# Setup order of a recommender kernel: the rest of W1 behind the first X0 transposes, VectorE one pair tile ahead, and chunk 1's gathers spaced by landings

## The chip, the cores and the metric

The kernel runs on one core of a Trainium2 chip. Its time is device microseconds, taken without a profile; the version before has three such runs. A trace was taken of one further, profiled execution. Engines are named as the profile names them: PE (TensorE matrix products), PEld (its weight loads), DVE (VectorE), ACT (ScalarE), POOL (GpSimd) and SP (SyncE, which here only issues transfers). `ACTq` and `SPq` are instructions with which ACT and SP issue transfers.

## The reference

1024 samples have 39 ids each, and each id picks a row of 16 values from one of 39 tables. Two interaction layers follow, whose sums over the 16 dimensions go with a third through a small network:

```python
def _cin_layer(X0, Xi, W, b):
    Wr = W.reshape(H, F0_, Fi)
    return jnp.einsum('hjk,bjd,bkd->bhd', Wr, X0, Xi) + b[None, :, None]
X0 = embedded_features                     # (1024, 39, 16), gathered from the tables
Xi = X0
for W, b in [(W0, b0), (W1, b1), (W2, b2)]:
    Xi = _cin_layer(X0, Xi, W, b)          # 128 maps
    res.append(Xi.sum(axis=2))
z = jnp.concatenate(res, axis=1)
h = jnp.concatenate([z, dense_ctx], axis=1)
h = jnp.maximum(h @ W_top1 + b_top1, 0.0)
h = jnp.maximum(h @ W_top2 + b_top2, 0.0)
y = h @ W_top3
```

The third layer is needed only as its sum over the dimensions, and the kernel forms it without the full product.

## The kernel before

The samples come in 8 chunks of 128. Every matrix product runs as three with operands split into an upper and a lower part (`_hi`, `_lo`): ACT rounds a value to the upper part, and DVE or POOL subtracts that to get the lower one.

**Setup.** POOL gathers chunk 0: 39 indirect transfers (L458), one per field, into `e_in`; `gathered` counts 16 per landing. SP loads W0 and W1. PE transposes W1 in ten pieces of 512 columns (`w1_turned`, L945) through `ring`, four banks of PSUM; ACT takes each piece's upper part (`w1_upper`, L552) and DVE its lower part (`w1_lower`, L773). Seven tiles of W0 are treated the same way. The semaphores `setup_ps`, `setup_hi` and `setup_lo` count finished batches, 12 in all (`SETUP`): two of W0's tiles, ten of W1.

**Step -1** makes layer 0 of chunk 0's first half. ACT moves the gathered rows into `e_both` (L583, L584), which also frees `e_in` (`e_mid_ready`). PE transposes X0 in four parts (L1048); ACT evacuates each to `x0_t` (L622, `x_t` in the trace) and signals `x0t_ready`. Copies of `x0_t` are then laid out by transfers: three into `x0_rep` (issued by ACT, L669) and 20 for seven pair tiles (issued by SP, L355; four slots for these first tiles, later two). For each of the seven pair tiles, DVE multiplies (L831, `pair_made`), ACT takes the upper part (L603, `pair_hi`), DVE the lower (L836, `pair_lo`), and PE adds six products to `l0_ps` (L984 to L986). ACT's `x1_half` (L573) then writes `x1_hi` and raises `x1_hi_ready`; DVE adds `x1_lo` (L803). The loops over 16 dimensions d and 10 groups g only set the order: a step's work stands at its (d, g), as `MADE_MID` = 1 and `LO_MID` = 7 do for DVE's two operations and `HI_AT` = 7 for ACT's.

**Steps 0 to 7** run layer 1 for one chunk each: per dimension ten groups of three products (L1098 to L1100) into the four banks of `ring`, emptied in turn by ACT (L692) and DVE (L897). Beside that run the pair tiles still due, of which POOL makes tiles 7 and up: `multiply_pairs` (L489) and `lower_pairs` (L500). In step 0 DVE makes tile 7 of chunk 0, and POOL starts with tile 8. PE adds tile 8's products at group 3 and 5 of dimension 1.

**Gathers ahead.** POOL also gathers the following chunk. The table `GATHERS` spreads 39 gathers over the dimensions of a step. In step -1 no POOL product stands between them, so POOL issues 29 for chunk 1 back to back once `e_in` is free (`next_index`, L475); the ten left over come in step 0 as 3, 3, 2, 2.

Each engine runs its instructions in the order written; an instruction that waits holds back all behind it on its engine. Semaphores connect the engines.

Of the kernel before, what the change touches and what calls it, by code (L numbers as in the profile page):

```python
# [4 lines left out]
FIELDS, D, H = 39, 16, 128  # L5
# [4 lines left out]
def build_tower(nc, dense_ctx, ids, tables, W_top1, b_top1, W_top2, b_top2, W_top3, W0, b0, W1, b1, W2, b2, out):  # L10
    f32, f32r, i32 = mybir.dt.float32, mybir.dt.float32r, mybir.dt.int32
# [76 lines left out]
    FIRST_MADE = 7  # L88
# [34 lines left out]
    X2_WRITES = {13: 0, 2: 1, 6: 2}  # L123
    X2_LAST_AFTER, X0_AFTER = 9, 11
    X2_SLOTS = 8
    W1_PIECE, W1_FIRST = 2, 2
    W2_AT = ((10, 6), (11, 1), (11, 6), (12, 1), (12, 6), (13, 1), (13, 6), (14, 1), (14, 6), (15, 1))
    W2_OUT_AT = [(d, g + 3) for d, g in W2_AT]
    QUARTERS = 4
# [2 lines left out]
    with ctx:  # L132
# [323 lines left out]
        def _(pool):  # L456
# [15 lines left out]
            def step(c, odd, layer1, following, previous, mlp, gathers):  # L472
                def next_index():
                    pool.wait_ge(gathered, 16 * FIELDS * (c + 2))
                    nc.gpsimd.tensor_copy(idx[:, :], ids_sb[:, c + 2, :]).then_inc(idx_ready, 1)  # L475
                    pool.wait_ge(idx_ready, c + 3)
                    pool.wait_ge(e_mid_ready, c + 2)

                def multiply_pairs(chunk, i):

                    half, t = TILE[i]
                    n = TILES * chunk + i
                    rows = ROWS_OF[t]
                    products, loaded, count = pair_slot(chunk, i)
                    if isinstance(chunk, int) and chunk == 0 and i == PAIR_TILES + 1:
                        pool.wait_ge(pair_made, n)
                    after(pool, rep_in, 16 * PER_TILE * (2 * chunk + half + 1))
                    after(pool, loaded, count)
                    nc.gpsimd.tensor_tensor(products[0:rows, :], x0_rep[0:rows, :], products[0:rows, :],  # L489
                                            ALU.mult).then_inc(pair_made, 1)  # L490

                def lower_pairs(chunk, i):

                    n = TILES * chunk + i
                    rows = ROWS_OF[TILE[i][1]]
                    if isinstance(chunk, int) and chunk == 0 and i == PAIR_TILES + 1:
                        pool.wait_ge(pair_lo, n)
                    after(pool, pair_hi, n + 1)
                    after(pool, pair_used, n - 1)
                    nc.gpsimd.tensor_tensor(pairs_lo[0:rows, i % 2, :], pair_slot(chunk, i)[0][0:rows, :],  # L500
                                            pairs_hi[0:rows, i % 2, :].bitcast(f32),
                                            ALU.subtract).then_inc(pair_lo, 1)

                def make_block(g):
                    n = G_GROUPS * (c - 1) + g
                    if g == 0:
                        after(pool, xb_in, 16 * c)
                        pool.wait_ge(own_made, 3)
                    after(pool, g_ps, n - min(g, BLOCK_SLOTS - 1))
                    shape = [P, FIELDS, SAMPLES_PER_G]  # L510
                    nc.gpsimd.tensor_tensor(  # L511
                        blocks[:, g % BLOCK_SLOTS, 0:FIELDS, :],
                        xb[:, g, :].unsqueeze(2).to_broadcast(shape),
                        own[:, :].unsqueeze(1).to_broadcast(shape), ALU.mult).then_inc(block_made, 1)

                for d in range(D):
                    made = tile_made(c, d, layer1, following) if layer1 else None
                    if made:
                        multiply_pairs(*made)
                    if layer1 and following and d < INDEX_SLICE:  # L520
                        for f in range(FIELDS - LATE + sum(GATHERS[:d]), FIELDS - LATE + sum(GATHERS[:d + 1])):
                            gather(c + 1, f)
                    if gathers and d == INDEX_SLICE - 1:
                        next_index()
                    if gathers and d >= INDEX_SLICE:
                        for f in range(sum(GATHERS[INDEX_SLICE:d]), sum(GATHERS[INDEX_SLICE:d + 1])):
                            gather(c + 2, f)
                    if previous:
                        for r in range(G_GROUPS):
                            if G_AT[r][0] == d + 1:  # L530
                                make_block(r)
                    if layer1 and d == Z0_ADD_SLICE:
                        pool.wait_ge(z0_summed, 2 * (c + 1))
                        nc.gpsimd.tensor_tensor(z0[:, odd, :], z0_part[:, :], z0[:, odd, :],
                                                ALU.add).then_inc(z0_ready, 1)
                    if made:
                        lower_pairs(*made)
# [7 lines left out]
        def _(act):  # L545
# [11 lines left out]
            for q in range(SETUP_V):  # L557
# [4 lines left out]
                    last = nc.scalar.activation(v_hi[0:rows, t, :], ring[0:rows, batch % RING, i * H:(i + 1) * H],  # L562
                                                ACT.Copy)
                last.then_inc(setup_hi, 1)
            for q in range(W1_FIRST, GROUPS):
                w1_upper(q)

            def step(c, odd, layer1, following, previous, mlp, gathers):
# [55 lines left out]

                def side_work(d, g):

                    if following and layer1 and not previous and (d, g) in W2_OUT_AT:
                        q = W2_OUT_AT.index((d, g))
                        n = piece_width(q)
                        act.wait_ge(w2_ps, q + 1)  # L630
                        nc.scalar.activation(w2_t[:, BANK * q:BANK * q + n], side[:, q % 2, 0:n],
                                             ACT.Copy).then_inc(w2_ready, 1)
# [98 lines left out]
                act.wait_ge(y_ps, CHUNKS)  # L731
                nc.scalar.activation(y_row, side[0:1, 1, 0:P], ACT.Copy).then_inc(y_ready, 1)

            act.wait_ge(small_in, 48)
            act.wait_ge(bias_sums, 3)
            act.wait_ge(top_in, 96)
            steps(act, step, tail)

        @block.vector
        def _(dve):  # L740
# [38 lines left out]
            for t in range(PAIR_TILES):  # L779
# [6 lines left out]
                                               v_hi[0:rows, t, :].bitcast(f32), ALU.subtract)  # L786
                if t % 4 == 3 or t == PAIR_TILES - 1:
                    last.then_inc(setup_lo, 1)
            for q in range(W1_FIRST, GROUPS):
                w1_lower(q)  # L790
            dve.wait_ge(small_in, 48)
            nc.vector.tensor_scalar(b0_sum[:, :], b0_col[:, :], float(D), None, ALU.mult).then_inc(bias_sums, 1)
# [5 lines left out]
            def step(c, odd, layer1, following, previous, mlp, gathers):  # L798
# [8 lines left out]
                def z0_half(half):  # L807
# [3 lines left out]
                    else:  # L811
# [3 lines left out]
                        by_group(dst), l0_ps[:, :].rearrange("p (d b g) -> p b g d", b=SAMPLES_PER_G, g=G_GROUPS),  # L815
                        AX.X, ALU.add).then_inc(z0_summed, 1)

                def first_pairs(d, g):

                    made = tile_made(c, d, layer1, following)  # L820
                    made_at, lo_at = (8, 9) if d == D - 1 else (MADE_MID, LO_MID)
                    if made and g in (made_at, lo_at):
                        chunk, i = made
                        n = TILES * chunk + i
                        half, t = TILE[i]
                        rows = ROWS_OF[t]
                        products, loaded, count = pair_slot(chunk, i)
                        if g == made_at:
                            after(dve, rep_in, 16 * PER_TILE * (2 * chunk + half + 1))
                            after(dve, loaded, count)  # L830
                            nc.vector.tensor_tensor(products[0:rows, :], x0_rep[0:rows, :], products[0:rows, :],  # L831
                                                    ALU.mult).then_inc(pair_made, 1)
                        else:
                            after(dve, pair_hi, n + 1)
                            after(dve, pair_used, n - 1)
                            nc.vector.tensor_tensor(pairs_lo[0:rows, i % 2, :], products[0:rows, :],  # L836
                                                    pairs_hi[0:rows, i % 2, :].bitcast(f32),
                                                    ALU.subtract).then_inc(pair_lo, 1)

                def sum_terms(e, part):  # L840

# [16 lines left out]
                def side_work(d, g):  # L858
                    for half, chunk in halves(c, layer1, following):
                        if (d, g) == X1_LO_AT[half]:  # L860
                            x1_lower(chunk, half)
                    for half in range(2):
                        if layer1 and (d, g) == Z0_AT[half]:
                            z0_half(half)
                    if not layer1:
                        first_pairs(d, g)

                for d in range(D):
# [62 lines left out]
        def _(pe):  # L931
# [20 lines left out]
            for q in range(SETUP_V):  # L952
# [5 lines left out]
                    last = nc.tensor.transpose(ring[0:rows, batch % RING, i * H:(i + 1) * H], v_raw[:, x:x + rows],  # L958
                                               ident[:, :])
                last.then_inc(setup_ps, 1)  # L960
            for q in range(W1_FIRST, GROUPS):
                w1_turned(q)
            pe.wait_ge(top_in, 96)
            pe.wait_ge(bias_sums, 2)
# [5 lines left out]
            def step(c, odd, layer1, following, previous, mlp, gathers):  # L970
# [18 lines left out]

                def side_work(d, g):  # L990

                    for j in range(FIELDS):
                        if not previous or Z2_PLACES[j] != (d, g):
                            continue
# [84 lines left out]
                    if used and g in L0_AT[d]:  # L1079
                        layer0(*used, L0_AT[d].index(g) * BANK)  # L1080

                for d in range(D):
                    if layer1 and d % (D // 2) == 0:
                        k = 2 * c + d // (D // 2) + 1
# [18 lines left out]

            pe.wait_ge(bias_sums, 3)
            pe.wait_ge(e_cleared, 1)
            pe.wait_ge(setup_hi, SETUP)
            pe.wait_ge(setup_lo, SETUP)
            def tail():
                m = M1 // P - 1
                for k, z in enumerate((z0[:, CHUNKS % 2, :], g_t[:, FIELDS, :], z2_sb, dense_t[:, :])):  # L1110
# [91 lines left out]
```

## Time and profile before

| | us |
|---|---|
| three timed runs | 1361.97, 1360.40, 1358.06 |
| their median | 1360.4 |
| span of the profiled execution | 1393.5 |
| PE busy in that span | 1272.0 (91%) |
| DVE busy | 1087.9 (78%) |
| ACT busy | 1039.8 (75%) |
| POOL busy | 882.6 (63%) |

The profiled execution has no timed number of its own; its span, from the first to the last instruction, is 33.1 us above the median of the timed runs. In the page's strip of 40 slices the granted TensorE clock reads 7556 in the first four (tenths of full speed, a slice is 34.8 us) and 9 or more after; POOL's gathers fill its first three slices.

In the trace, `<-issue` behind an idle time means that nothing in the trace released the instruction, and `<-remote` that a semaphore did whose writer the trace does not name. A timeline row gives the start, the duration, the operation and, in brackets, the idle time before it on that engine and what ended it. PE durations overlap, so the pace of PE is read from the starts.

### The profile page before, as it was taken

The page shows a single profiled execution, that of the slowest core. Times are in us where ns is not written, and L with a number is a line of the kernel's source. Part 1 is how long each engine was busy: PE and PEld are TensorE (multiplying, and loading weights), DVE is VectorE, ACT ScalarE, POOL GpSimd, SP SyncE. Part 2 cuts the span into 40 slices and gives each one's busy share as a digit, 9 for nine tenths or more (in the row PEclk, how much of TensorE's full clock was granted, in tenths as well). Part 3 has the DMA queues.
Part 4 walks back from the last instruction along what each step waited for, and adds up shares of the span by engine and source line. Part 5 has one row for each costly group of instructions (what it writes and reads, how often), then busy time and mean ns, then how long its engine had stood idle before and what let it go on. Part 6 is the DMA issues. An engine that isn't in the chain of part 4 may idle for free.

```text
span 1393.5 us, 23236 instructions
## 1 busy us (share of the span) xinstructions
PE 1272.0 (91%) x6037; PEld 1041.9 (75%) x6037; DVE 1087.9 (78%) x2694; ACT 1039.8 (75%) x3353; POOL 882.6 (63%) x654
## 2 busy tenths in 40 slices
PE   2127999999999999999999999999999999999997
PEld 2115778777888878787887878787888888887876
DVE  3125898988888788888888888888888888988992
ACT  1114888888788887788777877888778887788772
POOL 6572777786776867686776877686776745363000
PEclk7556999999999999999999999999999999999999
DMA  4042522242233221242223221242232221240000
GB/s 147 10 107 56 139 63 62 75 99 52 62 75 89 57 58 48 68 100 52 65 72 82 57 67 48 68 96 56 56 81 78 58 64 46 65 98 25 16 16 16
DMA packets 71598, 92.39 MB, mean 66 GB/s; under 512 B 31745, under 2 KB 53762, under 8 KB 70306
## 3 DMA queue, kind: packets, MB, share of 16 engines
q1 hardware_dynamic: 61318, 87.75, 24.5%
q0 software_dynamic: 9984, 2.58, 2.0%
q8 instruction: 53, 0.87, 0.3%
q14 instruction: 87, 0.71, 0.2%
q10 hardware_dynamic: 156, 0.48, 0.1%
HBM read 21.03 MB, written 10.95 MB: 23 GB/s over the span
## 4 chain that ended last, share of the span: by engine, by line
PE 81%; DVE 5%; ACT 4%; another core or an unknown queue 4%; issue 4%; DMA 1%; ACTq 0%; POOL 0%; DVEq 0%; SPq 0%; POOLq 0%
PE ring L1098 19%; PE ring L1100 19%; PE ring L1099 18%; PE side L998 4%; PE side L1065 4%; PE l_ps L984 4%; PE l_ps L986 3%; PE l_ps L985 3%; ACT terms L692 2%; DVE x_s L852 2%; DVE terms L897 2%; PE side L1017 1%; PE side L1048 1%; PE side L1026 1%
## 5 line engine op out<-in xcount | busy, mean ns | idle before, releaser
L692 ACT ACTIVATE terms<-ring,e_both 128x128 f32<-128x128 f32 x2944 | 839.2, 403 | 214.4 <-PE ring L1100 180.2
L1098 PE MATMUL ring<-w_hi,x_hi 128*128 128x512 f32 (+1 forms) x1280 | 556.5, 435 | 15.8 <-ACT terms L692 8.7
L897 DVE SCALAR_TENSOR_TENSOR terms<-ring,e_both,terms 128x128 f32<-128x128 f32 x1792 | 507.9, 344 | 65.2 <-PE ring L1100 57.3
L1100 PE MATMUL ring<-w_hi,x_lo 128*128 128x512 f32 (+1 forms) x1280 | 499.1, 390 | 0.0
L1099 PE MATMUL ring<-w_lo,x_hi 128*128 128x512 f32 (+1 forms) x1280 | 497.2, 388 | 0.0
L852 DVE TENSOR_REDUCE x_s<-terms 128x32 f32<-128x800 f32 x512 | 489.1, 976 | 0.7 <-ACT terms L692 0.7
L500 POOL TENSOR_TENSOR pairs_lo<-pairs,pairs_hi 117x1024 fp32r<-117x1024 f32 (+1 forms) x104 | 250.1, 2404 | 231.7 <-ACT pairs_hi L603 226.7
L458 POOL DMA_INDIRECT e_in<-in_tbl,idx x312 | 302.1, 968 | 93.8 <-issue 70.6
L1098 PEld LDWEIGHTS ring<-w_hi,x_hi 128*128 128x128 f32 x1280 | 242.9, 190 | 74.4 <-ACT terms L692 17.7
L1100 PEld LDWEIGHTS ring<-w_hi,x_lo 128*128 128x128 f32 x1280 | 241.1, 188 | 50.5
L489 POOL TENSOR_TENSOR pairs<-x_rep,pairs 117x1024 f32<-117x1024 f32 (+1 forms) x104 | 250.3, 2406 | 36.4 <-DMA pairs<-x_t 35.4
L1099 PEld LDWEIGHTS ring<-w_lo,x_hi 128*128 128x128 f32 x1280 | 243.6, 190 | 39.3
L603 ACT ACTIVATE pairs_hi<-pairs 117x1024 fp32r<-117x1024 f32 (+1 forms) x109 | 119.9, 1100 | 23.8 <-issue 14.8
L889 DVE SCALAR_TENSOR_TENSOR terms<-ring,e_both,b_rows 128x128 f32<-128x128 f32 x128 | 44.9, 350 | 117.4 <-PE ring L1100 116.9
L984 PE MATMUL l_ps<-pairs_hi,v_hi 117*128 117x512 f32 (+1 forms) x224 | 95.2, 425 | 43.9 <-DVE pairs_lo L836 20.9
L998 PEld LDWEIGHTS side<-g_t,w_t 128*128 128x128 f32 x546 | 100.3, 188 | 22.3
L998 PE MATMUL side<-g_t,w_t 128*128 128x128 f32 x546 | 102.2, 273 | 0.0
L511 POOL TENSOR_TENSOR blocks<-xb,own 128x312 f32<-128x312 f32 x112 | 79.6, 731 | 26.3 <-PE side L1065 23.4
L986 PE MATMUL l_ps<-pairs_lo,v_hi 117*128 117x512 f32 (+1 forms) x224 | 90.9, 406 | 0.0
L985 PE MATMUL l_ps<-pairs_hi,v_lo 117*128 117x512 f32 (+1 forms) x224 | 90.8, 405 | 0.0
L984 PEld LDWEIGHTS l_ps<-pairs_hi,v_hi 117*128 117x128 f32 (+1 forms) x224 | 43.5, 194 | 59.3 <-issue 26.6
L1065 PE MATMUL side<-blocks,x_r 128*128 128x320 f32 x224 | 79.0, 434 | 0.1
(113 smaller groups left out, 655.8 us busy)
## 6 DMA issues: line engine op xcount, KB each, us to landing
pairs<-x_t SPq DMA_DIRECT2D x312, 156.0 KB
x_scratch<-x_s SPq DMA_DIRECT2D x32, 256.0 KB, 2.2
x_r<-x_scratch SPq DMA_DIRECT2D x7, 1024.0 KB
x_rep<-x_t SPq DMA_DIRECT2D x45, 156.0 KB
e_in<-in_tbl,idx POOLq DMA_INDIRECT x312
x_scratch<-e_both SPq DMA_DIRECT2D x8, 312.0 KB, 7.6
g_t<-in_L_rec_W SPq DMA_DIRECT2D x1, 2496.0 KB, 15.9
xb<-x_scratch SPq DMA_DIRECT2D x8, 312.0 KB
```

What stands on the lines that cost most here:

```text
L458: nc.gpsimd.indirect_dma_start(e_in[:, f, :], None, tables[f], bass.IndirectOffsetOnAxis(ap=idx[:, f:f + 1], axis=0)).then_inc(gathered, 16)
L489: nc.gpsimd.tensor_tensor(products[0:rows, :], x0_rep[0:rows, :], products[0:rows, :], ALU.mult).then_inc(pair_made, 1)
L500: nc.gpsimd.tensor_tensor(pairs_lo[0:rows, i % 2, :], pair_slot(chunk, i)[0][0:rows, :], pairs_hi[0:rows, i % 2, :].bitcast(f32), ALU.subt ...
L692: last = nc.scalar.activation(term(d, ACT_BEFORE[d][g] + i), twos(ring[:, (GROUPS * d + g) % RING, i * H:(i + 1) * H]), ACT.Copy, scale=sc ...
L852: last = nc.vector.tensor_reduce(twos(x2_s[:, d % X2_SLOTS, h]), terms[:, d % 2, a, 0:TERMS[d], :].rearrange("p a t b -> p a b t"), AX.X, ...
L897: nc.vector.scalar_tensor_tensor(out=acc, in0=y, scalar=scale_of(j, d), in1=acc, op0=ALU.mult, op1=ALU.add).then_inc(dve_unit, 1)
L984: nc.tensor.matmul(acc, v_hi[0:rows, t, :], p_hi, start=(t == 0), stop=False)
L998: last = nc.tensor.matmul(side[:, 0, 0:P], w2_t[:, j * H:(j + 1) * H], g_t[:, j, :], start=(j == 0), stop=(j == FIELDS - 1))
L1065: nc.tensor.matmul(side[:, r % 2, 0:SAMPLES_PER_G * GCOLS], x2_r[:, r, :], blocks[:, r % BLOCK_SLOTS, :, :].rearrange("p b j -> p (b j)"), ...
L1098: nc.tensor.matmul(acc, x1_hi[:, x], w1_hi[:, w], start=True, stop=False)
L1099: nc.tensor.matmul(acc, x1_hi[:, x], w1_lo[:, w], start=False, stop=False)
L1100: nc.tensor.matmul(acc, x1_lo[:, x], w1_hi[:, w], start=False, stop=True).then_inc(y_group, 1)
```

## The change

It edits the order of the setup in four places; the work itself stays, and no transfer or operation is added or removed.

W1's pieces 5 to 9 (transposes, uppers, lowers) move from the setup into step -1, to (6, 0): behind the first two X0 transposes and the layout transfers, ahead of the first pair tile. ACT's waits for the small inputs move there and to the start of step 0. PE's wait for all twelve setup batches moves to the start of step 0; ahead of step -1 it waits for seven.

DVE's order in step -1 becomes one tile ahead: product d, then the lower part of d - 1. POOL's 29 gathers in step -1 get waits: the first for `x0t_ready` (two parts evacuated), each of the first twelve for the landing of the one before, the thirteenth for `x1_hi_ready`.

```diff
@@ constants
-    W1_PIECE, W1_FIRST = 2, 2
+    W1_PIECE, W1_FIRST, W1_EARLY = 2, 2, 5
+    W1_REST_AT = (6, 0)
+    GATHERS_EARLY = 12
@@ POOL, step
                         for f in range(sum(GATHERS[INDEX_SLICE:d]), sum(GATHERS[INDEX_SLICE:d + 1])):
+                            if not layer1 and f == 0:
+                                pool.wait_ge(x0t_ready, 2)
+                            if not layer1 and f == GATHERS_EARLY:
+                                pool.wait_ge(x1_hi_ready, 1)
+                            if not layer1 and f < GATHERS_EARLY:
+                                pool.wait_ge(gathered, 16 * (FIELDS + f))
                             gather(c + 2, f)
@@ ACT (DVE with w1_lower and PE with w1_turned alike)
-            for q in range(W1_FIRST, GROUPS):
+            for q in range(W1_FIRST, W1_EARLY):
                 w1_upper(q)
...
+                    if not layer1 and (d, g) == W1_REST_AT:
+                        for q in range(W1_EARLY, GROUPS):
+                            w1_upper(q)
+                        act.wait_ge(small_in, 48)
+                    if layer1 and not previous and (d, g) == (0, 0):
+                        act.wait_ge(top_in, 96)
+                        act.wait_ge(bias_sums, 3)
...
-            act.wait_ge(small_in, 48)
-            act.wait_ge(bias_sums, 3)
-            act.wait_ge(top_in, 96)
             steps(act, step, tail)
@@ DVE, first_pairs
+                    if (d, g) == W1_REST_AT:
+                        for q in range(W1_EARLY, GROUPS):
+                            w1_lower(q)
+                    if g == MADE_MID and tile_made(c, d, layer1, following) and d < D - 1:
+                        first_product(d)
+                        if d > FIRST_MADE:
+                            first_lower(d - 1)
+                    if (d, g) == (FIRST_MADE + PAIR_TILES, 0):
+                        first_lower(d - 1)
+                    if (d, g) == (D - 1, 8):
+                        first_product(d)
+                    if (d, g) == (D - 1, 9):
+                        first_lower(d)
@@ PE
+                if layer1 and not previous:
+                    pe.wait_ge(setup_hi, SETUP)
+                    pe.wait_ge(setup_lo, SETUP)
...
-            pe.wait_ge(setup_hi, SETUP)
-            pe.wait_ge(setup_lo, SETUP)
+            pe.wait_ge(setup_hi, SETUP - GROUPS + W1_EARLY)
+            pe.wait_ge(setup_lo, SETUP - GROUPS + W1_EARLY)
```

`first_product` and `first_lower` hold the same two operations with the same waits that `first_pairs` had (L831, L836).

POOL, from its first index copy to tile 8's lower part, before. `e_in<-in_tbl,idx` is a gather; a number behind x counts equal instructions in a row.

```order
L467 COPY idx<-ids_sb 128x39 [waits ids_in]
L458 DMA e_in<-in_tbl,idx 128x16 [waits idx_ready]
L458 DMA e_in<-in_tbl,idx 128x16 x38
L475 COPY idx<-ids_sb 128x39 [waits gathered]
L458 DMA e_in<-in_tbl,idx 128x16 [waits e_mid_ready,idx_ready]
L458 DMA e_in<-in_tbl,idx 128x16 x28
L489 TENSOR_TENSOR pairs<-x_rep,pairs 117x1024 [waits pair_in0,rep_in,pair_made]
L458 DMA e_in<-in_tbl,idx 128x16 x3
L500 TENSOR_TENSOR pairs_lo<-pairs,pairs_hi 117x1024 [waits pair_used,pair_hi,pair_lo]
```

And now:

```order
L469 COPY idx<-ids_sb 128x39 [waits ids_in]
L460 DMA e_in<-in_tbl,idx 128x16 [waits idx_ready]
L460 DMA e_in<-in_tbl,idx 128x16 x38
L477 COPY idx<-ids_sb 128x39 [waits gathered]
L460 DMA e_in<-in_tbl,idx 128x16 [waits x0t_ready,gathered,e_mid_ready,idx_ready]
L460 DMA e_in<-in_tbl,idx 128x16 [waits gathered] x11
L460 DMA e_in<-in_tbl,idx 128x16 [waits x1_hi_ready]
L460 DMA e_in<-in_tbl,idx 128x16 x16
L491 TENSOR_TENSOR pairs<-x_rep,pairs 117x1024 [waits pair_in0,rep_in,pair_made]
L460 DMA e_in<-in_tbl,idx 128x16 x3
L502 TENSOR_TENSOR pairs_lo<-pairs,pairs_hi 117x1024 [waits pair_used,pair_hi,pair_lo]
```

The run of 29 gathers is split into 12 that wait for landings and 17 that stand between `x1_hi_ready` and tile 8's product (L489 before, L491 now). The three gathers between that product and its lower part stay.

ACT, from W1's later uppers to the first pair tiles, before:

```order
L552 ACTIVATE w_hi<-ring 128x512 [waits setup_ps] x7
L552 ACTIVATE w_hi<-ring 128x384 [waits setup_ps]
L583 ACTIVATE e_both<-e_in 128x624 [waits top_in,gathered,bias_sums,small_in]
L584 ACTIVATE e_both<-e_in 128x304
L622 ACTIVATE x_t<-side 58x512 [waits x0t_ps] x2
L669 DMA x_rep<-x_t 39x1024 [waits x0t_ready]
L669 DMA x_rep<-x_t 39x1024 x2
L603 ACTIVATE pairs_hi<-pairs 117x1024 [waits pair_made] x2
```

And now:

```order
L560 ACTIVATE w_hi<-ring 128x512 [waits setup_ps] x3
L591 ACTIVATE e_both<-e_in 128x624 [waits gathered]
L592 ACTIVATE e_both<-e_in 128x304
L630 ACTIVATE x_t<-side 58x512 [waits x0t_ps] x2
L684 DMA x_rep<-x_t 39x1024 [waits x0t_ready]
L684 DMA x_rep<-x_t 39x1024 x2
L560 ACTIVATE w_hi<-ring 128x512 [waits setup_ps] x4
L560 ACTIVATE w_hi<-ring 128x384 [waits setup_ps]
L611 ACTIVATE pairs_hi<-pairs 117x1024 [waits pair_made,small_in]
L611 ACTIVATE pairs_hi<-pairs 117x1024 [waits pair_made]
```

X0's move and its first two evacuations (L583, L622; now L591, L630) and the three layout transfers pass the last five uppers of W1.

DVE at the first pair tiles, before:

```order
L831 TENSOR_TENSOR pairs<-x_rep,pairs 117x1024 [waits pair_in0,rep_in]
L836 TENSOR_TENSOR pairs_lo<-pairs,pairs_hi 117x1024 [waits pair_hi]
L831 TENSOR_TENSOR pairs<-x_rep,pairs 117x1024 [waits pair_in1,rep_in]
L836 TENSOR_TENSOR pairs_lo<-pairs,pairs_hi 117x1024 [waits pair_hi]
L831 TENSOR_TENSOR x_r<-x_rep,x_r 117x1024 [waits pair_in2,rep_in]
L836 TENSOR_TENSOR pairs_lo<-x_r,pairs_hi 117x1024 [waits pair_used,pair_hi]
```

And now, with W1's last lowers ahead of them:

```order
L785 TENSOR_TENSOR w_lo<-ring,w_hi 128x512 [waits setup_hi] x4
L785 TENSOR_TENSOR w_lo<-ring,w_hi 128x384 [waits setup_hi]
L837 TENSOR_TENSOR pairs<-x_rep,pairs 117x1024 [waits pair_in0,rep_in]
L837 TENSOR_TENSOR pairs<-x_rep,pairs 117x1024 [waits pair_in1,rep_in]
L847 TENSOR_TENSOR pairs_lo<-pairs,pairs_hi 117x1024 [waits pair_hi]
L837 TENSOR_TENSOR x_r<-x_rep,x_r 117x1024 [waits pair_in2,rep_in]
L847 TENSOR_TENSOR pairs_lo<-pairs,pairs_hi 117x1024 [waits pair_hi]
L837 TENSOR_TENSOR x_r<-x_rep,x_r 117x1024 [waits pair_in3,rep_in]
```

Each product (L837) now stands ahead of the lower part (L847) of the tile before it.

## Rows read from the trace of the kernel before

**Rows 1.** The windows view: busy time of each engine by stretch of the span, in us.
```profile
core 0: us, PE busy (x) PEld busy (x) DVE busy (x) ACT busy (x) POOL busy (x), PEclk, DMA share, GB/s
67.10:126.00 58.90, 19.89 (x51) 13.43 (x51) 18.12 (x15) 9.59 (x11) 28.18 (x28) 0.56 0.35 83
126.00:142.00 16.00, 16.00 (x59) 12.86 (x60) 11.32 (x29) 11.19 (x37) 10.32 (x7) 0.82 0.31 79
142.00:1354.00 1212.00, 1191.78 (x5677) 978.95 (x5675) 1031.50 (x2559) 996.53 (x3254) 804.20 (x572) 1.00 0.27 66
```

**Rows 2.** Waits of PE, 142 to 1354 us: total us, times, longest.
```profile
PE ring L1098 <- ACT terms L692: 8.7, 15, 1.4
```

**Rows 3.** Waits of all engines, 0 to 130 us.
```profile
ACT w_hi L552 <- remote: 40.0, 6, 10.6
...
ACT x_t L622 <- remote: 19.4, 1, 19.4
```

**Rows 4.** Timeline, chunk 0's last gather to X0's move: start us, us, operation, [idle before].
```profile
51.96 0.95 POOL L458 DMA_INDIRECT e_in<-in_tbl,idx  x1 [0.30 <-issue]
54.31 0.22 POOL L475 COPY idx<-ids_sb 128x39 int32<-128x39 int32 x1 [1.40 <-DMA e_in<-in_tbl,idx]
...
63.33 0.72 ACT L583 ACTIVATE e_both<-e_in 128x624 f32<-128x624 f32 x1 [3.27 <-issue]
...
65.17 0.97 POOL L458 DMA_INDIRECT e_in<-in_tbl,idx  x1 [10.65 <-ACT e_both L584]
...
66.52 0.59 ACT L622 ACTIVATE x_t<-side 58x512 f32<-58x512 f32 x1 [0.26 <-PE side L1048]
```

**Rows 5.** Timeline of step -1: first tiles, SP's loads, second half of X0.
```profile
67.14 4.02 ACTq L669 DMA_DIRECT2D x_rep<-x_t  x3
...
78.18 1.23 DVE L831 TENSOR_TENSOR pairs<-x_rep,pairs 117x1024 f32<-117x1024 f32 x1 [14.94 <-issue]
79.44 1.06 ACT L603 ACTIVATE pairs_hi<-pairs 117x1024 fp32r<-117x1024 f32 x1 [12.33 <-issue]
80.53 1.26 DVE L836 TENSOR_TENSOR pairs_lo<-pairs,pairs_hi 117x1024 fp32r<-117x1024 f32 x1 [1.12 <-issue]
81.71 1.21 DVE L831 TENSOR_TENSOR pairs<-x_rep,pairs 117x1024 f32<-117x1024 f32 x1
...
87.74 0.61 PE L1048 MATMUL side<-ident,e_both 128*65 128x128 f32 x4
...
94.44 2.13 SPq L355 DMA_DIRECT2D x_r<-x_t  x2
...
107.15 0.59 ACT L622 ACTIVATE x_t<-side 58x512 f32<-58x512 f32 x1 [19.42 <-remote]
```

**Rows 6.** Timeline of POOL in step -1: a gather beside VectorE, and the last.
```profile
81.78 1.96 POOL L458 DMA_INDIRECT e_in<-in_tbl,idx  x1 [0.30 <-issue]
...
102.58 0.94 POOL L458 DMA_INDIRECT e_in<-in_tbl,idx  x1 [0.30 <-issue]
```

**Rows 7.** Timeline, the end of step -1 and the first groups of step 0.
```profile
123.40 1.11 ACT L573 ACTIVATE x_hi<-l_ps,b_col 128x1024 fp32r<-128x1024 f32 x1 [4.27 <-PE l_ps L986]
...
125.98 0.76 PE L1098 MATMUL ring<-w_hi,x_hi 128*128 128x512 f32 x1 [2.62 <-DVE x_lo L803]
...
130.76 2.46 POOL L489 TENSOR_TENSOR pairs<-x_rep,pairs 117x1024 f32<-117x1024 f32 x1 [27.24 <-DMA pairs<-x_t]
134.36 1.11 ACT L603 ACTIVATE pairs_hi<-pairs 117x1024 fp32r<-117x1024 f32 x1
...
135.31 1.98 ACT L692 ACTIVATE terms<-ring,e_both 128x128 f32<-128x128 f32 x7
...
137.54 0.39 PE L1098 MATMUL ring<-w_hi,x_hi 128*128 128x512 f32 x1
```

**Rows 8.** Timeline of step 0: the last late gather and what waits for it.
```profile
159.87 0.95 POOL L458 DMA_INDIRECT e_in<-in_tbl,idx  x1 [0.30 <-issue]
...
167.63 0.72 ACT L583 ACTIVATE e_both<-e_in 128x624 f32<-128x624 f32 x1 [2.90 <-DMA e_in<-in_tbl,idx]
```

More of the change, by code:

```diff
@@ L788, in _ @@
                     last.then_inc(setup_lo, 1)
-            for q in range(W1_FIRST, GROUPS):
+            for q in range(W1_FIRST, W1_EARLY):
                 w1_lower(q)
@@ L816, in z0_half @@
                         AX.X, ALU.add).then_inc(z0_summed, 1)
-                def first_pairs(d, g):
[L820 to L838, printed above, removed]
@@ new lines, in first_product @@
+                def first_product(d):
+                    chunk, i = tile_made(c, d, layer1, following)
+                    rows = ROWS_OF[TILE[i][1]]
+                    products, loaded, count = pair_slot(chunk, i)
+                    after(dve, rep_in, 16 * PER_TILE * (2 * chunk + TILE[i][0] + 1))
+                    after(dve, loaded, count)
+                    nc.vector.tensor_tensor(products[0:rows, :], x0_rep[0:rows, :], products[0:rows, :],
+                                            ALU.mult).then_inc(pair_made, 1)
@@ new lines, in first_lower @@
+                def first_lower(d):
+                    chunk, i = tile_made(c, d, layer1, following)
+                    n = TILES * chunk + i
+                    rows = ROWS_OF[TILE[i][1]]
+                    after(dve, pair_hi, n + 1)
+                    after(dve, pair_used, n - 1)
+                    nc.vector.tensor_tensor(pairs_lo[0:rows, i % 2, :], pair_slot(chunk, i)[0][0:rows, :],
+                                            pairs_hi[0:rows, i % 2, :].bitcast(f32),
+                                            ALU.subtract).then_inc(pair_lo, 1)
@@ L864, in side_work @@
                             z0_half(half)
-                    if not layer1:
+                    if not layer1 and following:
                         first_pairs(d, g)
@@ L960, in _ @@
                 last.then_inc(setup_ps, 1)
-            for q in range(W1_FIRST, GROUPS):
+            for q in range(W1_FIRST, W1_EARLY):
                 w1_turned(q)
@@ L990, in side_work @@
                 def side_work(d, g):
+                    if not layer1 and (d, g) == W1_REST_AT:
+                        for q in range(W1_EARLY, GROUPS):
+                            w1_turned(q)
                     for j in range(FIELDS):
```

## The prediction

> **What bounds the kernel now.** I read the windows by stage first. From 142 to 1354 us PE is busy 1191.78 of 1212.00 us at a granted clock of 1.00 [rows 1]; the largest wait of PE in it is 8.7 us in 15 pieces, for ACT's terms [rows 2]. The change touches nothing there, so those 1212 us stay. What it can move lies before 142 us: the stretch 67.1 to 126 us, where PE is busy 19.89 of 58.90 us, and the first 16 us of step 0, where PE has no idle time but a mean clock of 0.82.
>
> The table of waits names two long ones in the setup, both of ACT and both with a releaser that the trace does not name: 40.0 us before W1's uppers in six pieces, and 19.4 us before one evacuation of X0 [rows 3]. The timeline places them. Chunk 0's last gather lands by 54.31 us, and X0's move, which could have begun then, begins at 63.33 us because ACT still works off W1's uppers [rows 4]: 9.0 us. Later PE turns X0's third part at 87.74 to 88.35 us, and ACT takes it at 107.15 us [rows 5], 3.6 us after the last of 29 gathers was issued (102.58 + 0.94) [rows 6]. With only two gathers issued, the second evacuation came 0.26 us after it was free to, released by PE [rows 4]. In this trace, then, signals from PE to ACT come late while POOL issues many gathers in a row.
>
> The central question is whether the timed runs hold these waits. The profiled span is 33.1 us above the median. The two waits cost the span 9.0 and about 17.3 us (19.4 less the roughly 2 us that DVE's chain would have needed anyway), 26.3 in all. Nothing else before 142 us is as large, and a stretch with PE 98% busy leaves little room to be shorter unprofiled. I take it that most of the 33.1 us is these two waits, and that they belong to the profiled execution.
>
> Two sentences of the Trainium skill stand beside this, and the sum does without them. "Runtime: NRT & Kernel Launch", section "The ~15µs preamble/postamble breakdown", gives a profile total about 6.2 us more than the reported time, whatever the kernel; by it some 27 of the 33.1 us are left, close to my 26.3, though no row here shows that part. "NOTIFIC — the notification-queue block", section "7.1 Overflow: three behaviours, one of which stalls the engine", says that the unit which writes the records holds back its producers rather than lose one; by it a late signal could be the recording's own, which the trace agrees with as far as the late ones fall beside many gathers, and does not prove.
>
> **The change part by part**, as the timed runs would have it. S is the start of layer 1, 125.98 us in this trace [rows 7].
>
> *W1's last five pieces.* Moved behind the layout transfers, they need five uppers of 0.60 us, as many lowers and 19 transposes. ACT and DVE stand idle 12.3 and 14.9 us ahead of the first pair tile [rows 5], while the transfers land, so I cost the work at 0. If the cover were gone, five uppers would cost 3.0 us. What the move gains is the 9.0 us, and only where ACT really waits; without late signals ACT would have been done with W1 before the gathers landed. Taken 0, bounds 0 and -9.0.
>
> *One tile ahead.* Before, product to product takes 3.53 us (78.18 to 81.71): product 1.23, upper 1.06, lower 1.26. DVE alone needs 1.23 + 1.26 = 2.49, so six steps save at most 6 x 1.04 = 6.2 us. Against that, SP's last tile loads are issued at 94.44 to 96.57 us [rows 5]; from the first product on, the old chain without the long wait reaches the last product at 78.18 + 6 x 3.53 = 99.4 us, only 2.8 us later. What is late next is SP's loads. Bounds 0 and -6.2; I take -2.5, near the loads, since spaced gathers may let them go a little sooner.
>
> *The gathers' waits.* The first twelve now cost a landing each. A quiet one took 54.31 - 51.96 = 2.35 us [rows 4]; one in step 0 took 167.63 - 159.87 = 7.76 us [rows 8]. From the first one's release at 67.14 us to `x1_hi_ready` (124.51 in this trace [rows 7], less 17.3 and 2.5) are 37.6 us, or 3.1 us for each of twelve. Up to 3.1 us they hide entirely. I take that, being nearer to the quiet row; each us above it would move the rest back by 12 us. As lower bound stands 0, as upper bound 12 x 4.7 = 56 us, which I hold unlikely since in step 0 the landing shared the queues with more.
>
> Behind the thirteenth gather's wait for `x1_hi_ready` are sixteen more, then tile 8's product. `x1_hi_ready` comes at S - 1.47 (123.40 + 1.11). A gather takes 0.95 + 0.30 = 1.25 us of POOL [rows 4], so seventeen end at S - 1.47 + 21.25 = S + 19.8. The product needs 2.46 us: S + 22.2; before, it ended at S + 7.2 [rows 7]. ACT's upper of tile 8 waits for it, with the terms of dimension 0's group 7 behind it in ACT's order: 1.11 for the upper and 4/7 of 1.98, or 1.13, for the terms, so that bank is free at S + 24.6, hand-overs of 0.1 us among them. PE wants it for dimension 1's second group, which began at S + 11.56 (137.54) [rows 7]. PE stalls 13.0 us there, and all the terms, PE's main work and every later step with it. Nothing takes this back, since PE has no slack later [rows 1]. Were gathers cheaper unprofiled, by their 0.30 us of issue, seventeen would save 5.1 us: bounds 8 and 13.
>
> *The clock.* Where PE stood idle two thirds of the time, the granted clock was 0.56; in the 16 us that follow, 0.82 with PE busy throughout [rows 1], which costs 16 x 0.18 = 2.9 us. A stall of 13 us puts PE back into such a state: once more 2.9 us. Bounds 0 and 2.9; I take 2.9.
>
> *Waits put off* (`top_in`, `bias_sums`, the last setup batches) end long before step 0; 0.
>
> The trap that the Trainium skill names in "SBUF — State Buffer", section "SBUF: two separate sides", bears on the paced gathers: GpSimd cannot write a gather's descriptors while VectorE runs a two-port operation. The trace has a row for it, 1.96 instead of 0.95 us beside a VectorE product at 81.71 [rows 5, 6]; twelve such would lengthen the early part by 12 us, which the upper bound above contains.
>
> Sum: -2.5 + 13.0 + 2.9 = +13.4 us, against the median since no removed wait of the profile is in it: 1360.4 + 13.4 = 1373.8, or 1374 us. With its bounds (-6.2 + 8 + 0 up to 0 + 13 + 2.9, and half of twelve gathers 1 us late each) its own range is 1363 to 1384.
>
> **The rivals.**
>
> *The waits are in the timed runs too* (faster). Then -9.0 - 17.3 - 2.5 + 13.0 + 2.9, and since seventeen gathers still run in a row beside PE's first groups, ACT's terms come late by some 4 us more: -8.9 us, 1351 us, with 1346 to 1356 around it. For it: the trace shows them plainly, and a semaphore that is late holds ACT for real in that execution. Against it: 33.1 us would have no other home.
>
> *They cancel.* Half the waits, or gathers that cost POOL less and a one-ahead order worth its full 6.2 us, against the same stall: within 4 us of 1360. The two bounds nearest to zero, -6.2 and +8, leave +2.
>
> *The stall doesn't come.* If PE's group 1 of dimension 1 did not stand behind tile 8's upper, 26 to 29 us would be free with the waits real: 1333 us. The order of ACT speaks against it: the upper stands ahead of group 7's terms [rows 7].
>
> *The early gathers are slow* (slower still): at 4.1 us a landing the burst starts 12 us later and PE's stall grows to 25: 1386 us. It decides from 3.1 us a landing on. I hold it within the forecast's upper end.
>
> **How the numbers follow.** Forecast, with its slow tail, 0.56; the waits are real 0.26; they cancel 0.14; no stall 0.04. Of this kernel 0.3% (4.1 us) can be told from no change. Faster takes the second and the fourth, 0.30; within 0.3% the third, 0.14; slower the first, 0.56. The time is 1374; the range reaches down to the heart of the faster case, 1348, and up to the forecast's own end, 1384.
>
> **What the profile after would show.** X0's move soon after the landing at about 54 us, and no 19 us before the third evacuation, by either case; so its span may be shorter than 1393.5 us by 26.3 + 2.5 - 15.9 = 13 us even where the time is longer. That would be the plainest sign that the profile held waits that the timed runs do not. POOL: twelve gathers some 3 us apart, seventeen at 1.25 us from `x1_hi_ready`, then tile 8's product some 20 us behind layer 1's start. PE: one idle piece of about 13 us before dimension 1's group 1, ended by ACT's terms, and the clock low behind it. The forecast is wrong if that piece is under 5 us, or if the time falls by more than 4 us with it in place; then the unnamed waits are real.

## The result, and the profile after

The changed kernel takes 1382.0 us (median of four runs, 1380.52 to 1384.96), the kernel before 1359.2 us beside it: a ratio of 1.0173, with a 95% interval of 1.0150 to 1.0196. It is 22.8 us slower. The profiled execution ran 1380.52 us with a span of 1378.7 us, so its trace shows a normal run. The profiled span fell from 1393.5 us while the time rose, as the prediction said it might.

First the windows of the changed kernel, cut at 97.0 (just behind layer 1's first product on PE, which starts at 95.78), at the start and end of PE's idle piece (107.7, 131.8), and where the clock is back (140.0); columns as in [rows 1].

```profile
core 0: us, PE busy (x) PEld busy (x) DVE busy (x) ACT busy (x) POOL busy (x), PEclk, DMA share, GB/s
0.00:54.00 54.00, 8.21 (x35) 7.32 (x35) 10.92 (x62) 5.53 (x14) 37.94 (x46) 0.68 0.34 97
54.00:97.00 43.00, 22.63 (x80) 17.16 (x81) 20.84 (x20) 14.17 (x19) 9.80 (x10) 0.70 0.45 113
97.00:107.70 10.70, 10.66 (x37) 7.86 (x36) 7.76 (x19) 5.32 (x17) 4.64 (x5) 0.80 0.33 82
107.70:131.80 24.10, 0.05 (x1) 0.00 (x0) 0.00 (x0) 2.14 (x6) 19.05 (x19) 0.58 0.07 6
131.80:140.00 8.20, 8.19 (x27) 6.31 (x28) 5.39 (x13) 5.46 (x18) 7.42 (x6) 0.78 0.25 57
140.00:1378.70 1238.70, 1218.12 (x5860) 1004.89 (x5858) 1040.44 (x2581) 1005.12 (x3283) 801.77 (x571) 1.00 0.27 65
```

The fourth stretch is the loss: 24.1 us in which PE and DVE do nothing, ACT has 2.1 us of work, the transfer engines are busy 7%, and only POOL works, 19 us of it.

The waits of the changed kernel from 0 to 180 us name the chain backwards (total, times, longest):

```profile
POOL e_in L460 <- DMA e_in<-in_tbl,idx: 34.2, 11, 5.0
...
PE ring L1131 <- ACT terms L707: 26.9, 3, 24.1
ACT pairs_hi L611 <- POOL pairs L491: 25.4, 1, 25.4
```

PE waits for ACT's terms, ACT for POOL's product of tile 8, and POOL had waited for eleven landings (the thirteenth gather waits for `x1_hi_ready` alone, so the twelfth landing holds nothing). POOL's timeline of the changed kernel shows the last steps:

```profile
58.63 0.97 POOL L460 DMA_INDIRECT e_in<-in_tbl,idx  x1 [4.40 <-ACT x_t L630]
64.58 0.94 POOL L460 DMA_INDIRECT e_in<-in_tbl,idx  x1 [4.97 <-DMA e_in<-in_tbl,idx]
...
101.22 0.94 POOL L460 DMA_INDIRECT e_in<-in_tbl,idx  x1 [1.75 <-DMA e_in<-in_tbl,idx]
105.09 0.94 POOL L460 DMA_INDIRECT e_in<-in_tbl,idx  x1 [2.93 <-DMA e_in<-in_tbl,idx]
106.34 0.95 POOL L460 DMA_INDIRECT e_in<-in_tbl,idx  x1 [0.30 <-issue]
...
126.31 0.94 POOL L460 DMA_INDIRECT e_in<-in_tbl,idx  x1 [0.30 <-issue]
127.28 2.35 POOL L491 TENSOR_TENSOR pairs<-x_rep,pairs 117x1024 f32<-117x1024 f32 x1
```

Twelve gathers stand from 58.63 to 105.09 us, (105.09 - 58.63) / 11 = 4.2 us apart. Seventeen follow at 1.25 us, and tile 8's product comes behind them. ACT and PE answer at the other end, the changed kernel's rows for [rows 7]:

```profile
93.20 1.11 ACT L581 ACTIVATE x_hi<-l_ps,b_col 128x1024 fp32r<-128x1024 f32 x1 [3.00 <-PE l_ps L1013]
...
129.66 1.06 ACT L611 ACTIVATE pairs_hi<-pairs 117x1024 fp32r<-117x1024 f32 x1 [25.38 <-POOL pairs L491]
130.62 2.94 ACT L707 ACTIVATE terms<-ring,e_both 128x128 f32<-128x128 f32 x11
```

```profile
95.78 0.76 PE L1131 MATMUL ring<-w_hi,x_hi 128*128 128x512 f32 x1 [2.62 <-DVE x_lo L815]
...
131.81 0.80 PE L1131 MATMUL ring<-w_hi,x_hi 128*128 128x512 f32 x1 [24.05 <-ACT terms L707]
```

`x1_hi` was ready at 94.31 us, but the seventeen gathers began at 106.34 us: 12 us of the stall come from the landings, 12 from the burst behind them; the experiments below take the two apart.

### The profile page after: what moved, and what is told of

The parts are those of the page before. It is cut to its first block, busy times and chain, and to the rows that moved or that the text cites. A ratio compares the mean times of both kernels' runs of the same rounds, so it can differ in the third digit from the quotient of the medians.

```text
span 1378.7 us, 23238 instructions
## 1 busy us (share of the span) xinstructions
PE 1267.9 (92%) x6037; PEld 1043.5 (76%) x6037; DVE 1085.3 (79%) x2694; ACT 1037.7 (75%) x3353; POOL 880.6 (64%) x654
## 4 chain that ended last, share of the span: by engine, by line
PE 81%; DVE 5%; issue 2%; POOL 2%; DMA 1%; ACT 1%; SPq 0%; DVEq 0%; POOLq 0%
PE ring L1131 19%; PE ring L1133 19%; PE ring L1132 19%; PE side L1095 4%; PE side L1028 4%; PE l_ps L1011 4%; PE l_ps L1013 3%; PE l_ps L1012 3%; DVE x_s L879 2%; DVE terms L924 2%; PE side L1047 2%; PE side L1078 1%; POOL e_in L460 1%; PE side L1056 1%; PE side L1183 1%
## 5 line engine op out<-in xcount | busy, mean ns | idle before, releaser
L491 POOL TENSOR_TENSOR pairs<-x_rep,pairs 117x1024 f32<-117x1024 f32 (+1 forms) x104 | 249.9, 2403 | 10.9 <-DMA pairs<-x_t 10.0
L513 POOL TENSOR_TENSOR blocks<-xb,own 128x312 f32<-128x312 f32 x112 | 79.3, 729 | 25.5 <-PE side L1095 24.1
```

## The experiments

Eleven runs put three questions: whether the timed runs ever held the unnamed waits of [rows 3], which edit costs the time, and what is left to gain. The kernel before ran beside each: its median was 1361.1 us for the first four, 1359.2 us for the next four and 1358.4 us for the last three.

**Without the gathers of step -1.** The kernel before, without 28 of its gathers; the counts that wait for landings are lowered by 28 x 16 = 448 to match, so this kernel computes chunk 1 from what lies in the buffer.

```diff
-                            gather(c + 2, f)
+                            if layer1 or f == 0:
+                                gather(c + 2, f)
```

> The kernel before, without 28 of the 29 gathers of chunk 1 in step -1 (only the first stays; chunk 1 then uses what lies in the buffer, and the counts of landings are lowered to match). Theory 1, the unnamed waits of ScalarE belong to the profiled execution of before and the timed runs don't hold them: the time stays at 1356 to 1361 us. Rival, the timed runs hold the 19.4 us wait behind the gathers: it goes with them, and the time falls by 13 to 19 us, to 1340 to 1346 us. By both, the third evacuation of X0 comes without a long wait in this profile.

Measured: 1362.7 us, ratio 1.0009 (0.9990 to 1.0027). That is 1.7 us above the expected range, and 1.6 us above the kernel before beside it. No 19 us are there to go. Theory 1 holds.

**W1's move alone.** All edits on W1 and the waits put off, without those on DVE's order and on the gathers.

> The kernel before, with W1's last five pieces behind the first X0 transposes and the waits put off; VectorE's order and the gathers as before. Theory 1: ScalarE is done with W1 before the gathers land, so the time stays within 3 us of before, 1356 to 1362 us. Rival, the waits are in the timed runs: 9 us less, 1350 us.

Measured: 1359.5 us, ratio 0.9993 (0.9983 to 1.0004). Its profile has 29 gathers in a row, and still PE releases the third evacuation after 1.64 us and the fourth after 0.34 us. The wait of 19.42 us in [rows 5] stood before the fourth; the prediction and the expectations call it the third. The third of that first trace was this one:

```profile
85.66 0.59 ACT L622 ACTIVATE x_t<-side 58x512 f32<-58x512 f32 x1 [1.65 <-issue]
```

**The gathers' waits alone.** The hunk on POOL of the change, nothing else.

> The kernel before, with the gathers' waits alone (first for two evacuations, twelve for a landing each, the thirteenth for x1_hi). The stall of the changed kernel (24.05 us before dimension 1's second group, ended by ScalarE's terms) comes from these waits: it must be here too, 18 to 26 us long, less by what layer 1 starts later; time 1378 to 1386 us. Rival, part of the loss comes from W1's move or VectorE's order: the time is under 1373 us.

Measured: 1381.8 us, ratio 1.0162 (1.0136 to 1.0187), with a stall of 20.14 us at the same place. The waits carry the whole loss. `x1_hi` came 2.4 us later than in the changed kernel (95.57 against 93.20), and layer 1 with it, so less of the gathers' lateness showed as a stall, and the time is the same.

**W1's move and one tile ahead, no gathers' waits.**

> The changed kernel without the gathers' waits: W1's move and VectorE one tile ahead. From the changed kernel's time less its stall and clock, 1382.0 - 24.1 - 1.8 = 1356.1: 1353 to 1359 us, no stall before dimension 1's second group. Rival, without spaced gathers the late signals come back in timed runs: 1365 us or more. Rival, the waits of before were real and go here in part: 1345 us or less.

Measured: 1358.1 us, ratio 0.9977 (0.9962 to 0.9993); PE has no stall before dimension 1's second group. Its longest wait for ACT's terms between 85 and 175 us is 2.2 us, at 141.59 us; the kernel before has one of 2.7 us at 144.19 us in its second profile.

**The kernel before, profiled again.**

> The kernel before, unchanged, profiled once more. Theory 1a, the unnamed waits of ScalarE belong to that one profiled execution: this one is without them, its span is 1356 to 1360 us, X0's move begins at about 54 us and the third evacuation at about 76 us, as in the run with W1's move alone. Theory 1b, every profiled execution of this order of work holds them: a span of 1390 us or more beside a time of 1360 us.

Measured: a span of 1360.4 us, 0.4 us beyond the expected range, at a time of 1363.3 us. The timeline of ACT in this second profile, to be held against 63.33 and 107.15 us in [rows 4, 5]:

```profile
54.10 0.72 ACT L583 ACTIVATE e_both<-e_in 128x624 f32<-128x624 f32 x1 [34.67 <-DMA e_in<-in_tbl,idx]
...
75.95 0.59 ACT L622 ACTIVATE x_t<-side 58x512 f32<-58x512 f32 x1 [1.39 <-PE side L1048]
...
78.05 0.59 ACT L622 ACTIVATE x_t<-side 58x512 f32<-58x512 f32 x1
...
96.44 1.11 ACT L573 ACTIVATE x_hi<-l_ps,b_col 128x1024 fp32r<-128x1024 f32 x1 [4.31 <-PE l_ps L986]
```

X0's move starts with the landing. The third evacuation is released by PE, and the fourth, at 78.05 us, follows without idle time; it is the one to hold against 107.15 us. No wait `<-remote` is left in this trace. POOL's rows of the same profile show that the gathers were as dense as ever, and where tile 8's product stood:

```profile
71.08 0.95 POOL L458 DMA_INDIRECT e_in<-in_tbl,idx  x1 [0.30 <-issue]
72.33 1.96 POOL L458 DMA_INDIRECT e_in<-in_tbl,idx  x1 [0.30 <-issue]
...
97.15 0.95 POOL L458 DMA_INDIRECT e_in<-in_tbl,idx  x1 [0.30 <-issue]
103.90 2.47 POOL L489 TENSOR_TENSOR pairs<-x_rep,pairs 117x1024 f32<-117x1024 f32 x1 [5.80 <-DMA pairs<-x_t]
```

The last early gather ends at 98.10 us; the product waits for a transfer, not for gathers.

**Nine gathers that wait instead of twelve.**

```diff
-    GATHERS_EARLY = 12
+    GATHERS_EARLY = 9
```

> The changed kernel with 9 in place of 12 gathers that wait for a landing each, so 20 behind x1_hi. Theory: twelve landings of 3.9 us (58.63 to 105.09 us in the changed kernel's trace) end 11 us after x1_hi is there (94.31), and hold the rest of the gathers and tile 8's product back. Nine end before it; the rest runs from 94.3 us on, 20 x 1.25 = 25.0, so the product starts at 119.3 instead of 127.28 us: PE's stall 24.05 - 8.0 = 16 us, time 1374 us (1371 to 1377). Rival, the number of gathers behind x1_hi alone sets the stall: three more gathers, 3.8 us more, 1386 us.

Measured: 1377.4 us (1371.33 to 1380.36), ratio 1.0118 (1.0081 to 1.0155). Three more gathers stood behind `x1_hi`, and the time fell; the rival would have it rise. POOL and PE of this kernel:

```profile
93.00 0.94 POOL L460 DMA_INDIRECT e_in<-in_tbl,idx  x1 [3.14 <-DMA e_in<-in_tbl,idx]
94.95 0.94 POOL L460 DMA_INDIRECT e_in<-in_tbl,idx  x1 [1.01 <-ACT x_hi L581]
...
120.33 2.35 POOL L491 TENSOR_TENSOR pairs<-x_rep,pairs 117x1024 f32<-117x1024 f32 x1
```

```profile
124.86 0.80 PE L1131 MATMUL ring<-w_hi,x_hi 128*128 128x512 f32 x1 [17.45 <-ACT terms L707]
```

The tenth gather waits for `x1_hi`, not for a landing. The product comes 7.0 us earlier than in the changed kernel and the stall is 6.6 us shorter. The time is at the upper end of what was expected, 0.4 us beyond it.

**Every second gather waits, two in flight.**

```diff
-                            if not layer1 and f < GATHERS_EARLY:
+                            if not layer1 and f < GATHERS_EARLY and f % 2 == 0:
```

> The changed kernel with only every second of the twelve early gathers waiting for the landings before it, two in flight. The early part is over before x1_hi; seventeen gathers from 94.3 us on end at 115.6 us, so the product starts 11.7 us earlier than in the changed kernel and PE's stall is 12.3 us, near the 13.0 of the prediction's sum; time 1370 us (1367 to 1373). Rival, two in flight land twice as late each: no change, 1382 us.

Measured: 1371.7 us (1369.57 to 1379.44), ratio 1.0103 (1.0058 to 1.0149). The thirteenth gather starts when `x1_hi` is there, and PE's stall is close to the 13.0 us of the prediction's sum:

```profile
96.06 0.94 POOL L460 DMA_INDIRECT e_in<-in_tbl,idx  x1 [0.36 <-ACT x_hi L581]
...
117.00 2.35 POOL L491 TENSOR_TENSOR pairs<-x_rep,pairs 117x1024 f32<-117x1024 f32 x1
```

```profile
121.53 0.80 PE L1131 MATMUL ring<-w_hi,x_hi 128*128 128x512 f32 x1 [13.10 <-ACT terms L707]
```

**Without the wait for `x1_hi`.**

> The changed kernel without the thirteenth gather's wait for x1_hi. Theory: that wait is long met when the twelfth has been issued (x1_hi at 94.31, the twelfth gather at 105.09 us), so nothing changes: a stall of 24 us, time 1382 us (1379 to 1385). Rival, the wait for x1_hi is what holds the gathers: 10 us less or more, 1372 us or below.

Measured: 1383.7 us, ratio 1.0190 (1.0157 to 1.0223), stall 24.0 us: no change, since the landings end later anyway.

Six kernels in one table, with PE's stall before dimension 1's second group in the profiled execution: without its stall, each time is within 2.5 us of 1359.2 us, the median of the kernel before beside the change.

| kernel | PE's stall, us | time, us | difference |
|---|---|---|---|
| no gathers' waits | 0 | 1358.1 | 1358.1 |
| every second of twelve | 13.1 | 1371.7 | 1358.6 |
| nine | 17.45 | 1377.4 | 1359.9 |
| twelve, without the other edits | 20.1 | 1381.8 | 1361.7 |
| twelve, no wait for `x1_hi` | 24.0 | 1383.7 | 1359.7 |
| the change | 24.05 | 1382.0 | 1358.0 |

**What is left to gain.** Three kernels without the landings' waits ran side by side.

> W1's move and VectorE one tile ahead, of the gathers' waits only the first (for two evacuations), 29 gathers back to back behind it. They start 2.7 us later than without it (58.6 instead of 55.9 us) and end at about 101 us; tile 8's product waited for its transfer until 103.9 us in the clean profile of before, so nothing is held back. Theory: as with no wait at all, 1355 to 1360 us, no stall. Rival, every wait on these gathers costs what it delays: 2.7 us more than without.

> The kernel before with VectorE one tile ahead alone. Theory: of the two edits that are left without the gathers' waits, this one carries all the gain, 1.4 us at x1_hi (95.01 against 96.44 us): 1356 to 1360 us, the same as with W1's move within 2 us. Rival, W1's move carries it: no gain here, 1360 us or more, 2 us above the run with both.

> W1's move and VectorE one tile ahead, the gathers as before, once more with five rounds: the candidate for a version that beats both. Theory: 1 to 4 us less than before, 1355 to 1359 us, interval of the ratio below 1. Rival, the first result was chance: ratio 1.000 with 1 inside the interval.

Measured: with the first wait kept 1357.5 us, ratio 0.9996 (0.9983 to 1.0010); one tile ahead alone 1357.3 us, 0.9991 (0.9980 to 1.0003); both edits without waits 1355.8 us, 0.9982 (0.9970 to 0.9994). The last is the version that beats both kernels, by 0.2%, and did so twice. Whether W1's move adds to it can't be told: alone neither edit differs from before, and the three intervals overlap. For the same reason the theory that one tile ahead carries all the gain is not shown, nor is a cost of the first wait ruled out: its kernel's median lies 1.6 us above the one without waits, between the theory's 0 and the rival's 2.7.

## Why the prediction was right, point by point

The direction was right, and so was the chain by which the time is lost: gathers in front of tile 8's product, ACT's terms behind it, PE's stall. The size was not: +13.4 us was forecast, +22.8 us measured. That 1382.0 us still lies in the range is partly luck. By the range's own terms its ends are 1360.4 - 6.2 + 8 = 1362.2 and 1360.4 + 15.9 + 6 = 1382.3 us, not 1363 and 1384, and the rival "the early gathers are slow", which is what took place, was priced at 1386 us, beyond the end that was said to hold it.

**The central question** came out as taken: the timed runs don't hold the unnamed waits. The runs without gathers (1362.7 us) and with W1 moved (1359.5 us) show it in the time, the second profile of before in the trace. The rival by which they were real (1351 us) is ruled out, and with it the late evacuation's 17.3 us and X0's 9.0 us as gains.

What the prediction said of their nature does not hold. It saw them where POOL issues many gathers in a row. Six more profiles (before again, W1 alone, one tile ahead alone, and the three with both edits and no waits for landings) have 29 gathers in a row and no late signal, and none of the twelve profiles taken after the first has a wait `<-remote`. They belonged to one execution. The sentence of the Trainium skill in "NOTIFIC — the notification-queue block", section "7.1 Overflow: three behaviours, one of which stalls the engine", remains a possible cause that no run here shows; recording alone does not bring the waits, since the second profile was recorded too. Their cause stays open.

The 6.2 us of the Trainium skill's "Runtime: NRT & Kernel Launch", section "The ~15µs preamble/postamble breakdown", are said of a profile's total, and no run here shows that quantity. The prediction set them against a span from the first to the last instruction, and there they did not serve: the time is longer than the span, by 1.8 us in the changed kernel's profiled run (1380.52 against 1378.7).

**W1's pieces at 0**: confirmed, ratio 0.9993. In the changed kernel they ran at 61.4 to 65 us, while the layout transfers landed.

**One tile ahead at -2.5**, with SP's loads late next: the last product moved from 89.83 us in the second profile of before to 87.40 us with both edits and no waits, and the start of `x1_hi` from 96.44 to 95.01 us, 1.4 us. The same kernel profiled again had it at 93.69 us, 2.8 us sooner; the 2.5 taken lies between. DVE's order in the first of these two profiles shows who is late now:

```profile
75.02 1.23 DVE L830 TENSOR_TENSOR x_r<-x_rep,x_r 117x1024 f32<-117x1024 f32 x1 [1.45 <-DMA x_r<-x_t]
...
81.36 1.23 DVE L830 TENSOR_TENSOR pairs<-x_rep,pairs 117x1024 f32<-117x1024 f32 x1 [1.40 <-DMA pairs<-x_t]
...
85.12 1.23 DVE L830 TENSOR_TENSOR pairs<-x_rep,pairs 117x1024 f32<-117x1024 f32 x1 [1.40 <-DMA pairs<-x_t]
```

The products wait for tile loads. Whether spaced gathers let these go sooner is not shown: with them `x1_hi` began at 93.20 us (the change), 93.57 us (nine) and 94.29 us (no wait for `x1_hi`), without them at 93.69 to 95.01 us in four profiles with one tile ahead.

**The burst of seventeen gathers at 13.0 us** was right in place and size: 13.1 us where the early part was over in time, each gather 1.25 us. Nothing was taken back later that the table above could show.

**The landings are the term that was mis-sized.** Taken was 3.1 us each, near the quiet row of [rows 4], which hid all twelve. Measured are 4.2 us from one gather to the next, between that and the 7.76 us of [rows 8]. From the first gather's release to `x1_hi` were 35.7 us (58.63 to 94.31), which eleven landings of 3.1 us and one gather fill; the early part ended 12 us later. The text had the price nearly right, 12 us for each us above 3.1 (eleven landings make it 11), and this case as its slow end ("at 4.1 us a landing ... PE's stall grows to 25").

The nearest row was the wrong choice. In the quiet row's window the transfer engines were busy 8%; the early gathers run beside 20 tile loads, with the engines busy 49% from the first to the twelfth. The changed kernel's windows, cut from one gather to the next, show that the landing goes with this load:

```profile
58.63:64.58 5.95, 2.47 (x13) 1.84 (x11) 2.51 (x5) 2.45 (x5) 0.97 (x2) 0.79 0.65 159
...
85.49:88.17 2.68, 1.33 (x5) 1.11 (x6) 2.68 (x4) 1.06 (x1) 0.97 (x1) 0.91 0.03 3
```

With the engines busy 65% the next gather came after 5.95 us, with 3%, in a gap of SP's loads, after 2.68 us. The nine between took 3.46 to 5.38 us at 30 to 59%, not in strict order. For the window of the paced gathers the first trace already gave a share of 0.35 [rows 1]. Gathers held by VectorE, the prediction's trap, are a small part: the twelve took 1.9 us more of POOL than 0.94 us each, not 12.

**The clock at 2.9**: in 131.8 to 140.0 us it was 0.78 with PE busy throughout, 8.2 x 0.22 = 1.8 us.

**The sum** with the measured terms: the stall was 11.05 us longer than taken (24.05 against 13.0), the clock cost 1.1 us less, and layer 1 started 3.2 us sooner than in the second profile of before (95.78 against 99.02) where 2.5 was taken. That makes 9.2 of the 9.4 us between +13.4 and +22.8, as near as single profiles allow. The forecast time was only 8 us low because it stood on 1360.4 us, and the kernel before took 1359.2 us beside the change.

The spans of the two profiles differ by less than the medians, 18.3 us (1378.7 against 1360.4). Layer 1 starts 3.2 us sooner; from there to dimension 1's second group 36.0 us against 11.7 (131.81 and 110.70), 24.4 more; from there to the end 1246.9 against 1249.7 us, 2.8 less. Both have the wait of PE for ACT's terms at X0's next move, 2.4 us at 166.96 us and 2.7 us at 144.19 us, so this wait does not make the 2.8. The execution of before was at 1363.3 us, 4 us above its median, the changed one 1.5 us below; behind its wait the granted clock was 0.74 for 5.9 us (144.1 to 150), against 1.00 in the changed kernel. Why it was lower there no run shows.

## What to carry to other kernels

An engine that runs in order pays a wait in front of everything behind it: before work that nobody needs yet is spaced out or put off, find the next instruction behind it that somebody does need, and its due time. Price a wait for a landing under the load that will surround it. And where a profiled span stands far above the timed runs, look for the waits that make up the difference, and do not count on removing them before a second profile shows them too.

## What the runs showed of the hardware

A gather that POOL starts while a VectorE operation with two inputs in SBUF is running ends no sooner than about 0.8 us after that operation. In the second profile of before, the gather at 72.33 us took 1.96 us and so ended at 74.29 us; the VectorE product beside it was:

```profile
72.26 1.21 DVE L831 TENSOR_TENSOR pairs<-x_rep,pairs 117x1024 f32<-117x1024 f32 x1
```

It ended at 73.47 us, 0.82 us before. In the changed kernel, the gather at 97.76 us took 1.70 us, beside a product that ended at 98.65 us: 0.81 us again. A gather that starts with such an operation or ahead of it is not held: 0.95 us at 71.08 us, beside the lower part that starts at 71.08 us. Nor is one beside W1's lower parts, whose one input lies in PSUM. With both edits and no waits (first profile) these were:

```profile
62.13 2.95 DVE L778 TENSOR_TENSOR w_lo<-ring,w_hi 128x512 fp32r<-128x512 f32 x5 [39.16 <-ACT w_hi L553]
```

The gather at 64.64 us started beside the last of them, took 0.94 us and ended 0.5 us after it.

The prediction cited for the hold the rule on two-port operations in the Trainium skill's "SBUF — State Buffer", section "SBUF: two separate sides". By the Trainium skill these products are no such operations (same page, section "Who interferes with whom"); it names there a second case, an operation with two SBUF inputs against GpSimd work that reads SBUF. The products have two such inputs, and the row of W1's lower parts, with one, agrees; what the gather reads while it is held no row shows.
